# First attention of a fused block: the softmax denominators from a float16 part and a bfloat16 rest made by GpSimd

## What is computed

```python
def proj(W, bias):
    y = jnp.tanh(states @ W + bias)
    return y.reshape(b, s, h, d).transpose(0, 2, 1, 3)
q, k, v = (proj(Wq, bq), proj(Wk, bk), proj(Wv, bv))
alpha = jnp.einsum('bhqd,bhkd->bhqk', q, k) / jnp.sqrt(jnp.float32(d))
causal = jnp.tril(jnp.ones((s, s), dtype=bool))
alpha = jnp.where(causal, alpha, jnp.finfo(jnp.float32).min)
alpha = jax.nn.softmax(alpha, axis=-1)
ctx = jnp.einsum('bhqk,bhkd->bhqd', alpha, v)
...
x = x + _layernorm(_L0_attn_ref(_layernorm(x, axis=-1), ...), axis=-1)
```

## Time and profile before

| What | Value |
|---|---|
| Median of 3 runs | 1804.86 us (1802.99 to 1805.49) |
| Profiled execution: its time | 1805.83 us |
| Profiled execution: its span | 1803.8 us |
| PE busy | 1644.7 us (91%) |
| DVE busy | 1438.8 us (80%) |
| ACT busy | 1223.1 us (68%) |
| POOL busy | 373.7 us (21%) |
| TensorE clock granted, mean | 0.947 |

### The profile page before, as it was taken

The page is one execution under the profiler, slowest core; times in us unless marked ns, Lnnn a source line. Parts: engine busy times, 40 slices in busy tenths (PEclk is TensorE's granted clock), DMA queues, the critical chain, the costliest instruction groups (busy, mean ns, idle before and its releaser), DMA issues. The chain is left out here.

```text
span 1803.8 us, 39594 instructions
## 1 busy us (share of the span) xinstructions
PE 1644.7 (91%) x14930; PEld 714.7 (40%) x14930; DVE 1438.8 (80%) x2115; ACT 1223.1 (68%) x1186; POOL 373.7 (21%) x505
## 2 busy tenths in 40 slices
PE   1499999999999999994999999999999999889995
PEld 1244444444444444442223233322232332366774
DVE  5067777888888888887898899897988999367888
ACT  4276666666666666652687778786777788756776
POOL 5011111333333333332321000100010212130004
PEclk8699999999999999995799899998999999979998
DMA  4311101100000000001101100110011010000001
GB/s 109 88 37 38 37 36 37 38 36 36 36 36 36 36 35 36 20 4 31 54 25 34 26 14 25 35 26 15 24 28 33 13 36 13 1 14 13 13 12 47
DMA packets 48154, 57.13 MB, mean 32 GB/s; under 512 B 9406, under 2 KB 34462, under 8 KB 48032
## 3 DMA queue, kind: packets, MB, share of 16 engines
q1 hardware_dynamic: 45920, 51.62, 9.2%
q10 hardware_dynamic: 2112, 3.86, 1.0%
HBM read 15.07 MB, written 10.49 MB: 14 GB/s over the span
## 5 line engine op out<-in xcount | busy, mean ns | idle before, releaser
L1464 DVE TENSOR_REDUCE arena<-psum 128x2 f32<-128x1024 f32 x490 | 581.5, 1219 | 62.0 <-PE psum L1113 57.7
L1290 ACT ACTIVATE arena<-psum 128x1024 f32<-128x1024 f32 x512 | 523.4, 1025 | 157.2 <-PE psum L1083 143.2
L642 ACT ACTIVATE arena<-psum 128x2048 f32<-128x2048 f32 (+1 forms) x160 | 273.4, 1708 | 232.6 <-PE psum L527 229.9
L1098 PE MATMUL psum<-arena 128*32 128x256 f32 x4096 | 337.2, 401 | 1.6 <-ACT arena L1304 0.7
L697 POOL TENSOR_SCALAR_AFFINE_SELECT arena<-arena 128x512 f32<-128x512 f32 (+1 forms) x160 | 167.9, 1067 | 571.3 <-ACT arena L642 571.3
L544 PE MATMUL psum<-arena,hs 128*64 128x512 f32 (+3 forms) x1536 | 283.0, 496 | 2.7 <-POOL arena L697 2.2
L1113 PE MATMUL psum<-arena 32*128 32x512 bf16 x1068 | 211.9, 412 | 25.1 <-ACT arena L1343 11.8
L527 PE MATMUL psum<-arena 64*128 64x512 f16 (+3 forms) x2304 | 216.3, 325 | 4.9 <-DVE arena L732 3.6
L1083 PE MATMUL psum<-arena 32*128 32x512 bf16 x1024 | 203.8, 395 | 4.5 <-issue 3.1
L732 DVE TENSOR_TENSOR arena<-arena 128x1024 f16<-128x1024 f32 x64 | 78.4, 1225 | 162.1 <-ACT arena L621 162.1
L544 PEld LDWEIGHTS psum<-arena,hs 128*64 128x64 f32 x1536 | 96.1, 136 | 144.8 <-issue 125.9
(11 more groups left out here) (202 smaller groups left out, 2115.5 us busy)
## 6 DMA issues: line engine op xcount, KB each, us to landing
arena<-arena SPq DMA_DIRECT2D x32, 512.0 KB, 3.0
arena<-arena SPq DMA_DIRECT2D x48, 128.0 KB, 2.3
arena<-latent_q SPq DMA_DIRECT2D x64, 64.0 KB, 1.9
arena<-latent_k SPq DMA_DIRECT2D x64, 64.0 KB, 2.0
arena<-arena SPq DMA_DIRECT2D x32, 96.0 KB, 2.6
X<-in_L_attn_states SPq DMA_DIRECT2D x4, 512.0 KB, 14.0
arena<-arena SPq DMA_DIRECT2D x32, 64.0 KB, 1.8
out_x<-X SPq DMA_DIRECT2D x4, 512.0 KB, 3.2
```

Source lines behind the costliest of these rows:

```text
L642: nc.scalar.activation(probs[g], SC[:, :, 0:WIDTH[g]], ACT.Exp, scale=DH ** -0.5).then_inc(exp_done, 1)
L1098: last = nc.tensor.matmul(OT[ROWS * c:ROWS * (c + 1), h * HALF // 2:(h + 1) * HALF // 2], v_cols[par][:, kt, 2 * pr + i, :], e_probs[u % 4 ...
L1290: nc.scalar.activation(e_probs[u % 4], src, ACT.Exp, scale=KD ** -0.5).then_inc(e_done, 1)
L1464: nc.vector.tensor_reduce(half_tops[:, kh, qt, 2 * pr:2 * pr + 2], src.rearrange("p (i c) -> p i c", i=2), AX.X, ALU.max).then_inc(top_don ...
```

## The change

After its mask of group 0, GpSimd now takes up the sums of the pair before (`split_sums(i-1)`). It waits for all of DVE's additions (`sum_lo`, `sum_hi`) and until PE has read the former parts (`den_done`; for the first pair, until the rows of 0 and -1 have been copied out, since the rest takes their place). It rounds the 2048 sums of each partition to float16 (`sums_hi`, in a free part of `hs`) and subtracts these from the sums into bfloat16 (`sums_lo`, in the last words of the arena). PE's denominators are then eight two-byte products that add up both parts in PSUM, in place of four float32 products. The last pair (31) keeps the old way. DVE may overwrite `sums[par]` once the split has read it, where it waited for PE before. Two memsets at the program's start fill the two-byte ones.

```diff
--- before.py
+++ after.py
@@ -156,6 +156,7 @@
         qk_bias = a1.take(2 * PAIRS).rearrange("p (t n) -> p t n", t=2)
         pick_bias = a1.take(P // 2, F16)
         ones = a1.take(DH)
+        ones_hi, ones_lo = a1.take(DH // 2, F16), a1.take(DH // 2, BF16)
         a0 = Arena(a1.at)
         w_in = a0.take(3 * H1 * DH).rearrange("p (t n) -> p t n", t=3)
         wo_in0 = a0.take(PAIRS * D).rearrange("p (n d) -> p n d", n=PAIRS)
@@ -254,11 +255,13 @@
                 nc.gpsimd.memset(bias_in, 0.0).then_inc(consts, 1)
                 nc.gpsimd.memset(mhalf[:, :], -0.5).then_inc(consts, 1)
                 nc.gpsimd.memset(ones, 1.0).then_inc(consts, 1)
+                nc.gpsimd.memset(ones_hi, 1.0).then_inc(consts, 1)
+                nc.gpsimd.memset(ones_lo, 1.0).then_inc(consts, 1)
                 nc.gpsimd.memset(zero_rows[0:ROWS, :], 0.0).then_inc(rows_filled, 1)
                 nc.gpsimd.memset(minus_rows[0:ROWS, :], -1.0).then_inc(rows_filled, 1)
                 pool.wait_ge(consts, 1)
                 nc.gpsimd.tensor_copy(identb[:, :], ident[:, :]).then_inc(consts, 1)
-                pool.wait_ge(consts, 6)
+                pool.wait_ge(consts, 8)
                 for b in range(B):
                     now = slice(b * T, (b + 1) * T)
                     pool.wait_ge(mv0, b + 1)
@@ -365,6 +368,8 @@
         spare = hs[:, :, :].rearrange("p t d -> p (t d)")
         vals = [spare[:, m * S:(m + 1) * S].rearrange("p (t c) -> p t c", t=T) for m in range(2)]
         rden = spare[:, 3 * S:4 * S]
+        sums_hi = spare[:, 2 * S:3 * S].bitcast(F16).rearrange("p (s q) -> p s q", s=2)
+        sums_lo = arena[:, ARENA - S:].bitcast(BF16).rearrange("p (s q) -> p s q", s=2)
 
         SC = bank(0, 4).rearrange("p (s c) -> p s c", s=2)
         PJ = bank(4, 2)
@@ -376,6 +381,7 @@
         vproj_done, vals_ready = sem("vproj_done"), sem("vals_ready")
         scores_done, exp_done, masked = sem("scores_done"), sem("exp_done"), sem("masked")
         sum_lo, sum_hi = sem("sum_lo"), sem("sum_hi")
+        sums_rounded, sums_split = sem("sums_rounded"), sem("sums_split")
         pv_done, den_done, den_read = sem("pv_done"), sem("den_done"), sem("den_read")
         out_copied, rden_ready, ctx_scaled, ctx_hi_done = (sem("out_copied"), sem("rden_ready"), sem("ctx_scaled"),
                                                            sem("ctx_hi_done"))
@@ -550,13 +556,19 @@
 
                     if not at_least_int(n, N1 - 2):
                         pe.wait_ge(tanh_done, 4 * (n + 2) + 4)
-                    pe.wait_ge(sum_lo, SUM_LO * (n + 1))
-                    pe.wait_ge(sum_hi, SUM_HI * (n + 1))
+                    if at_least_int(n, N1 - 1):
+                        pe.wait_ge(sum_lo, SUM_LO * (n + 1))
+                        pe.wait_ge(sum_hi, SUM_HI * (n + 1))
+                        parts = ((ones, sums[par]),)
+                    else:
+                        pe.wait_ge(sums_split, n + 1)
+                        parts = ((ones_hi, sums_hi), (ones_lo, sums_lo))
                     for half in range(2):
                         now = slice(half * HALF, (half + 1) * HALF)
-                        for s in range(2):
-                            last = nc.tensor.matmul(PJ[s * DH:(s + 1) * DH, now], ones, sums[par][:, s, now],
-                                                    start=True, stop=True, skip_group_check=True)
+                        for m, (one, part) in enumerate(parts):
+                            for s in range(2):
+                                last = nc.tensor.matmul(PJ[s * DH:(s + 1) * DH, now], one, part[:, s, now],
+                                                        start=(m == 0), stop=(m == len(parts) - 1), skip_group_check=True)
                         last.then_inc(den_done, 1)
 
                 def output(n, par):
@@ -713,8 +725,22 @@
                     nc.gpsimd.tensor_tensor(tile_rstd, tile_rstd, mhalf[:, 0:1], ALU.pow).then_inc(tile_pow, 1)
                     nc.gpsimd.tensor_copy(one_tile(acc, t), ob_b[:, :]).then_inc(tile_reset, 1)
 
+                def split_sums(n, par):
+
+                    wait_apart(pool, sum_lo, SUM_LO * (n + 1))
+                    wait_apart(pool, sum_hi, SUM_HI * (n + 1))
+                    if at_least(n, 1):
+                        wait_apart(pool, den_done, 2 * n)
+                    else:
+                        pool.wait_ge(rows_set, 16 * ROW_FILLS)
+                    nc.gpsimd.tensor_copy(sums_hi, sums[par]).then_inc(sums_rounded, 1)
+                    wait_apart(pool, sums_rounded, n + 1)
+                    nc.gpsimd.tensor_tensor(sums_lo, sums[par], sums_hi, ALU.subtract).then_inc(sums_split, 1)
+
                 def pair(i, par, last=False, norm=False):
                     mask(i, 0)
+                    if at_least(i, 1):
+                        split_sums(i - 1, 1 - par)
                     mask(i, 3)
                     mask(i, 4)
                     if norm:
@@ -770,7 +796,7 @@
                 def lo_first(i, par):
                     dve.wait_ge(masked, 3 * i + 1)
                     if at_least(i, 2):
-                        dve.wait_ge(den_done, 2 * (i - 1))
+                        dve.wait_ge(sums_split, i - 1)
                     p, v = probs[0], sums[par]
                     nc.vector.tensor_copy(v[:, :, 0:P], p[:, :, 0:P]).then_inc(sum_lo, 1)
                     nc.vector.tensor_tensor(v[:, :, P:HALF], p[:, :, HALF:7 * P], p[:, :, P:HALF], ALU.add).then_inc(sum_lo, 1)
```

## The result

The changed kernel takes 1833.84 us (median of 4 runs, 1828.97 to 1842.77), the kernel before 1803.92 us (4 runs). The ratio of the two is 1.018, with a 95% interval of 1.013 to 1.024. The profiled execution has a span of 1832.2 us, 28.4 more than before.

What follows compares the result with a forecast made beforehand. The prediction took a loop through PE, ACT and DVE's output addition to bound late pairs; holds beyond DVE's pauses add 33 us there and 2.4 in early pairs, 35 on 1805.83, so 1841 and a median of 1840, range 1816 to 1860.

Steps and rivals of the forecast that it cites:

- What bounds: Late pairs: a loop PE, ACT, DVE and back through DVE's output addition fills the 23.09 us, denominators not in it.
- One sign: Late pairs of the changed kernel: the context product of group 3 would still be released by GpSimd's mask.
- PE's saving: Denominators: two-byte products save 0.7 us of PE time; winnable 0.06 us in a late pair, up to 0.40 in an early.
- The holds: DVE additions beside GpSimd's split: held 1.64 us by the rounding and 3.83 by the subtraction, 5.5 us a pair.
- The rule's wording: DVE and GpSimd's shared SBUF ports as an exclusive lock: 5.97 us a pair, late pairs 44 us in place of 33.
- The late pair: 22 late pairs: 1.85 us of hold beyond DVE's pauses less 0.34 of mask relief, 1.5 us each, 33 us.
- The relief from the masks: Late pairs: mask of group 3 comes ahead of L793, giving back 0.34 us; the 0.64 at L808 and L810 stays.
- The early pair: Pairs 4 to 9: pauses swallow 5.2 of 5.5 us, leaving 0.4 us each, 2.4 us; pairs 1 to 3 at 0.
- The sum: Whole kernel: 33 + 2.4 = 35 us on the profiled 1805.83 us, so 1841; forecast for the median 1840.
- The pauses that take it all: Rival: DVE is held under 3.65 us a pair, nothing lost, early pairs win 0.40 us each, 1801 us; chance 0.10.
- A late GpSimd: Rival: the subtraction ends after 623.4, delaying group 3's mask and context product, 80 us more, 1885 us; chance 0.08.
- the new wait: PE's wait for GpSimd's split ahead of the denominators: costs nothing while GpSimd is less than 4.5 us late.

Runs made afterwards that it cites:

- products alone: Kernel before, with eight two-byte products of a constant tensor for the denominators and no split: late pair 23.10 us, ratio to before 0.999.
- before, output sooner: Kernel before, with DVE's output addition placed ahead of its last two hi_third additions: late pair 22.80 us, ratio 1.000, run again 0.996.
- the split unused: Changed kernel, GpSimd still splits but PE uses four float32 products of the unsplit sums: late pair 24.41 us, ratio to before 1.018.
- rounding alone: Changed kernel without GpSimd's subtraction, PE adding the rounded part twice: late pair 23.11 us, ratio to before 0.998.
- the fills: Changed kernel, three GpSimd memsets in place of rounding and subtraction, PE using float32 products of unsplit sums: late pair 23.10 us, ratio to before 1.000.

## Why the prediction was right, point by point

*What bounds.* Right. Without the split PE's saving moves the late pair by 0.01 us (products alone), and moving DVE's output addition forward moves it by 0.3 (before, output sooner). 99% of busy PE had pointed to the wrong engine. One sign came only in part: the mask of group 3 still releases the context product in 8 of 16 late pairs between 350 and 750 us of the changed kernel, in the others PE doesn't wait there, as in the pair above.

*PE's saving.* Forecast 0.7 us of PE time, measured 1.82 - 0.96 = 0.86; worth nothing in late pairs and at most 0.40 in early ones. Measured in the kernel before it is 0.01 and 0.33. In the changed kernel's late pairs PE gives it back in its two waits for DVE.

*The holds.* Forecast 1.64 + 3.83 us, measured against the lengths of before (1.21 and 0.41 us): 2.91 - 1.21 = 1.70 and 4.30 - 0.41 = 3.89, together 5.6. The estimate from an instruction of half the size held. The rule's wording (whole instructions, 5.97 us) was 0.4 us too much.

*The late pair.* Forecast + 1.5 us, measured 24.42 - 23.11 = + 1.31, for 22 pairs 29 us in place of 33. The relief from the masks was mis-sized and misplaced. I took 0.34 us at `hi_second` and nothing at `last_sums`. It was 2 x (1.381 - 1.275) = 0.21 at `hi_second`, with the mean of L793 from 328 to 790 us before, and 0.44 + 0.20 = 0.64 at `last_sums`. In return the mask now meets two small instructions: `add_tile` (L852) takes 484 ns and `scale_ctx` (L790) 1411, against the 292 and 1218 they took before, 0.39 us. The balance is 5.59 - 3.65 - 0.21 - 0.64 + 0.39 = 1.48. Some 0.14 more goes because each L758 now starts 0.07 us before the instruction ahead of it ends (639.54 against 639.61), where it stood behind a pause. That leaves 1.34, near the 1.31.

*The early pair.* Forecast + 0.4 us, measured + 0.76. This is the term that was most off. DVE's timeline in an early pair of the changed kernel shows masks on additions where there were none before (683 ns in the earlier trace rows):

```profile
217.76 1.12 DVE L834 TENSOR_TENSOR arena<-arena 128x512 f32<-128x512 f32 x1
218.81 0.89 DVE L836 TENSOR_TENSOR arena<-arena 128x512 f32<-128x512 f32 x1
...
231.14 2.78 DVE L819 TENSOR_TENSOR arena<-arena 128x1024 f32<-128x1024 f32 x2
```

I had allowed for it as a bound of 0.64 us and counted 0.1. It is 0.44 + 0.20 at `last_sums` and 2 x (1.36 - 1.24) = 0.24 at `hi_second`, 0.9 together. With the 0.3 that the pauses leave that would be 1.2; some 0.2 of the difference to 0.76 is the same overlap, at the three pauses that are gone, and the rest is in terms of 0.1 us and less.

*The sum.* Forecast 33 + 2.4 = 35 us for the stage, measured 718.6 - 683.9 = 34.7. Distance by distance it is 7 x 0.76 = 5.3 up to pair 9, 0.2 from there to pair 10, 20 x 1.31 = 26.3 among the late pairs, and 2.9 from pair 30 to 31 (22.38 in place of 19.44). Pair 3, which I had put at 0, lost as much as the six after it. The late pairs together are 29.4 for a forecast of 33 and the early ones 5.3 for 2.4; that the two misses cancel is luck. The median moved by 29.9 us and the profiled span by 28.4. In the profiles the difference of 6.3 us lies outside the stage. From the last output addition to the end of the span it takes 968.6 us where it took 973.3, and the change does nothing there. The first one comes at 145.0 us where it was 146.6; it comes at 148.0 in the kernel with the split unused, so this tells nothing. I had said that 0.2% can be told from no change; with four runs each the interval is 0.5% to either side, so the time bears out a loss of about 30 us, and only the profiles tell its terms apart.

*The rivals.* The pauses that take it all need a hold of under 3.65 us; rounding alone is that case, and there they do. A late GpSimd isn't seen, the split is done 3.3 us before PE asks. That GpSimd's length as such, or the new wait, costs in the late pairs is excluded by the fills.

## What to carry to other kernels

Before giving GpSimd work beside a busy DVE, add the lengths of its instructions that read SBUF to DVE's busy time wherever DVE adds or subtracts two SBUF tensors, and compare with DVE's pauses that follow in the loop. Here a hold of 1.7 us within pauses of 3.65 was free, and of a hold of 5.6 us what lay beyond them was paid, less what the masks gave back. Look at DVE's copies too, for in the fills' kernel writes held one up. GpSimd's own idle time says nothing about it. A PE that is 99% busy can still wait in a loop through another engine; ask what ends its shortest waits, and what the product after next waits for, before taking products away.

## What the runs showed of the hardware that I had not expected

The holds of one long instruction and of four short ones are the same to 0.1 us (3.89 and 4 x 0.96), with strict turns in between. A DVE copy got no such turn: it was held for 5 us through three GpSimd fills that read nothing. And the spread of the times is not where the change is: two profiles of one kernel (before, output sooner, and again) have stages of 678.9 and 678.8 us, but spans of 1790.7 and 1804.8 us, with mean granted TensorE clocks of 0.955 and 0.942. For a change in one stage the distance of two instructions on the trace can tell 1 us, where the times of the whole left the 5 us of the swap in doubt.
